# Products with the values in pairs of steps, scores four and maxima ten steps ahead, in an attention and mixture-of-experts block

## The reference

```
scores = (q @ k^T + q_rope @ k_rope^T) * scale      # 4 batches x 16 heads, 512 x 512
attn   = softmax(scores, axis=-1)
out    = (attn @ v) laid out by token @ Wout        # then x = x + ga * out
h      = layernorm(x) * (1 + cb) + sb
x      = x + gb * (experts(h) + shared(h))
```

## Time and profile before

| | us |
|---|---|
| median of 3 runs | 1003.52 (1001.63 to 1004.96) |
| the profiled execution | 1001.45 |
| its span | 999.6 |

### The profile page before, as it was taken

The page is one execution under the profiler, slowest core; times in us unless marked ns, Lnnn a source line. Parts: engine busy times, 40 slices in busy tenths (PEclk is TensorE's granted clock), DMA queues, the critical chain, the costliest instruction groups (busy, mean ns, idle before and its releaser), DMA issues.

```text
span 999.6 us, 19865 instructions
## 1 busy us (share of the span) xinstructions
PE 869.2 (87%) x6994; PEld 738.8 (74%) x6994; DVE 732.2 (73%) x1586; ACT 573.6 (57%) x1072; POOL 657.4 (66%) x625
## 2 busy tenths in 40 slices
PE   5788999999999999999999997649973999999940
PEld 5656777778788888788888786439862899999940
DVE  5777999887978788786879784676842566666648
ACT  1345777778787878887788886523310344444420
POOL 3555878878797888887887985515676355555530
PEclk9999999999999999999999999859985899999975
DMA  8661613233522345232334254333222333333337
GB/s 296 230 133 30 177 31 82 61 64 78 157 50 74 65 98 161 47 83 49 75 67 149 49 159 157 102 76 104 95 107 100 114 118 116 120 116 124 112 122 299
DMA packets 65756, 111.20 MB, mean 111 GB/s; under 512 B 16917, under 2 KB 43292, under 8 KB 63820
## 3 DMA queue, kind: packets, MB, share of 16 engines
q1 hardware_dynamic: 46905, 69.24, 26.0%
q10 hardware_dynamic: 11843, 22.84, 6.5%
q0 software_dynamic: 6912, 17.84, 4.6%
HBM read 46.06 MB, written 39.58 MB: 86 GB/s over the span
## 4 chain that ended last, share of the span: by engine, by line
PE 58%; DVE 11%; POOL 11%; DMA 10%; issue 5%; ACT 3%; SPq 0%; POOLq 0%; ACTq 0%; DVEq 0%
PE bank L680 12%; PE bank L682 11%; PE bank L681 10%; DMA slots<-h,slot_i 7%; PE bank L860 7%; PE bank L1076 7%; POOL p_lo L1912 5%; PE bank L837 4%; POOL turns L1890 2%; PE bank L1048 2%; POOL slots L1969 2%; PE bank L934 2%; DVE nmax L1250 1%; DVE turns L1224 1%; DVE turns L1223 1%
## 5 line engine op out<-in xcount | busy, mean ns | idle before, releaser
L1912 POOL TENSOR_TENSOR p_lo<-p_f,p_hi 128x512 f16<-128x512 f32 x256 | 329.6, 1299 | 46.7 <-ACT p_f L1647 45.8
L1644 ACT ACTIVATE p_hi<-bank,log_up 128x512 f16<-128x512 f32 x256 | 176.1, 688 | 108.2 <-PE bank L682 99.0
L1250 DVE TENSOR_REDUCE nmax<-bank 128x1 fp32r<-128x512 f32 x256 | 174.4, 686 | 86.1 <-PE bank L837 83.0
L1647 ACT ACTIVATE p_f<-bank,log_up 128x512 f32<-128x512 f32 x256 | 175.1, 684 | 15.2 <-POOL p_lo L1912 15.2
L860 PEld LDWEIGHTS bank<-vals,p_hi 128*128 128x128 f16 x2048 | 110.4, 98 | 59.6 <-POOL p_lo L1912 28.6
L860 PE MATMUL bank<-vals,p_hi 128*128 128x66 f16 x2048 | 138.7, 194 | 15.3 <-POOL p_lo L1912 15.1
L1230 DVE TENSOR_TENSOR qk<-rows_f,qk 128x512 fp32r<-128x512 f32 (+1 forms) x128 | 132.6, 1036 | 2.2
L1890 POOL TENSOR_TENSOR turns<-turns 128x512 f32<-128x512 f32 x64 | 90.4, 1414 | 66.0 <-DVE turns L1224 66.0
L680 PE MATMUL bank<-qk 128*128 128x512 f32 x256 | 122.2, 477 | 6.2 <-issue 4.9
L860 PE MATMUL bank<-vals,p_lo 128*128 128x66 f16 x1024 | 121.1, 193 | 0.0
L837 PE MATMUL bank<-qk 128*128 128x512 f32 x256 | 104.2, 410 | 3.8 <-DVE nmax L1250 3.4
(11 more groups left out here) (228 smaller groups left out, 2099.3 us busy)
## 6 DMA issues: line engine op xcount, KB each, us to landing
rows_f<-turns SPq DMA_DIRECT2D x64, 256.0 KB, 3.9
slots<-pad ACTq DMA_DIRECT2D x4, 2880.0 KB, 10.1
h<-slots SPq DMA_DIRECT2D x80, 144.0 KB
w_hi<-parts SPq DMA_DIRECT2D x16, 512.0 KB, 8.3
rows_f<-kl_f SPq DMA_DIRECT2D x32, 192.0 KB, 3.0
w_raw<-in_w ACTq DMA_DIRECT2D x4, 1408.0 KB, 11.8
h_dram<-h_hl SPq DMA_DIRECT2D x3, 1024.0 KB, 4.8
qk<-lat_st SPq DMA_DIRECT2D x16, 192.0 KB, 4.3
```

The costliest lines, as they stand in the source:

```text
L1250: dve.tensor_reduce(nmax[:, k % MAXES:k % MAXES + 1], max_bank[q % 2][:], AX_X, ALU.max, negate=True)\
L1644: act.activation(p_hi[:, u % TB, :], score_bank[u % 2][:], ACT.Exp, bias=log_up[:, 0:1], scale=SCALE)
L1647: act.activation(p_f[:, u % 2, :], score_bank[u % 2][:], ACT.Exp, bias=log_up[:, 0:1], scale=SCALE)\
L1912: pool.tensor_tensor(p_lo[:, u % TB, :], p_f[:, u % 2, :], p_hi[:, u % TB, :], ALU.subtract).then_inc(s_pl, 1)
```

## The change

TensorE makes the products with the values of steps `u` and `u + 1` together, at each even `u`, and none at odd `u`. The scores run four steps ahead in place of three, on TensorE, ScalarE and GpSimd; the maxima ten in place of nine, on TensorE and VectorE. Nothing else is changed, and no instruction is added or taken away.

```
-AHEAD = 3
-MAX_AHEAD = 2 * TB + 1
+AHEAD = 4
+MAX_AHEAD = 2 * TB + 2
...
             for w in range(AHEAD):
                 score(w)
             pe.wait_ge(spared, 3)
-            score_max(2 * TB)
+            for k in range(2 * TB, MAX_AHEAD):
+                score_max(k)
             aux(("kl", 2))
             pe.wait_ge(m_ev, 4)
             pe.wait_ge(v_l, 1)
             for u in range(UNITS):
-                weigh_values(u)
+                if u % 2 == 0:
+                    weigh_values(u)
+                    weigh_values(u + 1)
                 if u + AHEAD < UNITS:
                     score(u + AHEAD)
                 if u + MAX_AHEAD < UNITS:
...
             low_rows(2, 1)
             low_rows(2, 0)
-            row_max(2 * TB)
+            for k in range(2 * TB, MAX_AHEAD):
+                row_max(k)
             dve.wait_ge(p_hhi, NB)
```

## The result

The changed kernel took 1016.07 us (1014.14 to 1018.2), the kernel before 1003.78 us (1001.63 to 1004.96) in the same comparison: ratio 1.0134, interval 1.0111 to 1.0157. It is 1.3% slower. The prediction said 982.7 us, 976 to 997, and faster; the truth lies outside on the other side, where the prediction had put 0.08.

A forecast was written before the change was run, and what follows sets the result against it. TensorE's order of work was taken to bound the attention loop. Shorter score entries (10.1 us) plus removed waits on low probabilities (10.7) gave 20.8 us off the 1003.52 median: 982.7 us, range 976 to 997.

The forecast's parts named there:

- The entries of S: TensorE, 126 odd steps: first score product no longer follows short value products, 0.08 us each, 10.1 us saved.
- S: TensorE: the three score products of one step, 0.31 + 0.23 + 0.24 us from start to start.
- W: TensorE: the twelve products with the values of one step, 0.38 us; an ordinary entry shows a 0.22 us wait.
- M: TensorE: the one product for the maxima in a step, 0.23 us.
- rival B: TensorE: the 0.08 us per S does not come back; 992.8 us, chance 0.11.
- Queues: SP's queue: odd head's row of maxima, right behind the turned rows, lands in 1.9 us, hidden with 1.5 left.
- Rival E: SP's queue, 31 pairs: row of maxima lands late behind 256 KB; 15.5 us, 998, or some 1,033; chance 0.10.
- The 10.7 us of waits of W: Scores four ahead: of 15.2 us lost waiting for GpSimd's low probabilities, 10.7 go and 4.5 stay.
- Its three places in the batches: Once per batch four tiny GpSimd instructions delay the low products: 1.8 us lost each before, 1.5 after.
- Pressure of the pairs: W of odd steps wanted 0.38 us behind the even one, less room for scores and exponentials; taken as 0.
- rival C: Lost time moves: VectorE as late as before, odd W meets its low product; 993.4 us, chance 0.17.
- Maxima ten ahead: Extra S and M ahead of the loop hide in TensorE's 2.00 us wait; uncovered, 1.01 us once.

The follow-up runs named there:

- kernel 1: Changed kernel with the products with values one step at a time again, scores four and maxima ten ahead kept: 1021.07 us, ratio 1.0168.
- 10: Changed kernel, row of maxima first on SP's queue, GpSimd's first rotary sum one later: 997.72 us; also unpaired 999.99; paired with adds and deviations later 998.41.
- 9: Changed kernel with the row of maxima first on SP's queue, plus second adding of rows and deviations one step later: 997.14 us, ratio 0.9897.
- first kernel of 10: Changed kernel, still paired, with row of maxima first on SP's queue and GpSimd's first rotary sum one later: 997.72 us, ratio 0.9918.
- 6: Kernel before, scores three and maxima nine ahead, with value products of u-1 and u together at each odd u: 998.47 us, ratio 0.9954.
- 8: GpSimd's first rotary sum one later: in the kernel before with value products paired at odd steps 993.26 us; alone in the kernel before 996.0 us.
- 7: Changed kernel with row of maxima first on SP's queue and GpSimd's first rotary sum two steps later: paired 1005.14 us, unpaired 1004.58 us.
- experiment 2: Changed kernel with the odd head's row of maxima issued ahead of the turned rows on SP's queue: 1000.98 us, ratio 0.9971.

## Why the prediction was wrong, by its own steps

**The entries of S: right.** The page of after gives

```profile
L680 PE MATMUL bank<-qk 128*128 128x512 f32 x256 | 113.4, 443 | 20.5 <-issue 13.8
```

443 ns in the mean, 0.43 forecast, 479 in the unpaired kernel 1. (479 - 443) x 256 = 9.2 us for 10.1. From start to start, in the trace of after from 88 to 600 us outside the stretches at half clock, the median is 0.314 us in 102 places behind W, 0.231 in 67 behind L682 and 0.235 in 38 behind M. So rival B is out: behind 66-column products the first product of S costs more. The Trainium skill (TensorE: Matmul & The Clock Gate, Step-by-step: what each phase is for) would have the next weights load under the running product, and by that alone the term would be 0; these runs go against it there. That it is the load that costs the 0.08 was not shown by itself.

**Queues: the step that failed.** It said of the row of maxima "Hidden, with 1.5 us left". Its issue right behind the turned rows was foreseen, 0.6 us behind them. What was wrong is that 1.9 us, the median landing, was taken for every pair, and the times of one pair for all. Behind the 256 KB most rows of odd heads took 3.4 to 4.4 us, in the pair above 6.0. Rival E had this very mechanism, and priced it at 15.5 us: the waits of L680 on "issue" and on line 1233 grew by 20.4 - 5.5 = 14.9 us. That the two numbers agree is chance. It wasn't 0.5 us in each of 31 pairs but twelve waits: three of 2.3 to 2.7 us behind landings of 6.0 to 6.4, one of 4.2 behind 8.3 (in before it was 2.8, behind 8.2), and smaller ones between. With the clock behind them the late rows cost some 21 us, and not 15. Its chance of 0.10 was the error: the 1.9 of the earlier trace rows is a median over 64 issues. The instructions of L563 show how far it reaches, before and then after:

```profile
DMA to landing us min/median/max: 1.9/1.9/8.2
```
```profile
DMA to landing us min/median/max: 1.9/2.3/8.3
```

**The 10.7 us of waits of W: half right.** Four ahead does take them away where W is single (kernel 1: 5.9 us in 23). In pairs the second W waits: of the 11.5 us in 13 times, 10.9 in 10 times stand before a W right behind another, where the ordinary 0.22 does not arise. The prediction let 4.5 stay, so 7.0 too few. Its three places in the batches are there, right behind the deviations, with 1.8 us each. What it missed are the seven others, 5.5 us: it followed the low product of step 8p+9 through one pair, and there GpSimd's sum, in five of the seven an adding of rows as well (L1902), stands close ahead. Putting the sum one later took 9.2 of the 14.8 us away (10), the adds and deviations 3.7 (9).

**The granted clock: missing from the sum.** The earlier trace rows show 1.00 for the loop of before, and the prediction priced a late transfer at the lateness alone. Behind four of the new waits the clock was halved, 6.6 us. The Trainium skill (TensorE: Matmul & The Clock Gate, Part 1: The HAM clock gate) says that the array's clock is gated to half when TensorE idles and recovers with work; this trace agrees, 0.50 from inside a wait of 2.20 us to 3 us behind it, and shows that single waits inside a dense loop are enough. Not each does it: in kernel 1 a wait of 2.86 us (551.70 to 554.56) left the clock at 1.00 for the 3.4 us behind it, while in the first kernel of 10 it fell to 0.50 at 104.69, behind one of 1.46 us (102.36 to 103.82).

**Pressure of the pairs, rival C: partly right.** It was put at 0. In four comparisons of kernels with and without them the pairs gained 5.0 (after against 1), 5.5 (6 against before), 2.7 (8) and 2.3 us (10), and nothing with the sum two later (7). Never 10. The signs that C named, the same number of waits at even steps, did not come: W waited 13 times for 51. What grows with pairing, where the old waits are gone, are M's waits for reductions and S's. That fits the part of C on VectorE's pace; it was seen beside the edits and not changed by itself.

**Maxima ten ahead: no loss of its own shown.** Ahead of the loop it cost nothing, the first W starts at 86.32 against 87.18.

The account, from 980.65 forecast for the profiled execution to 1016.95: row of maxima 14.9, clock 6.6, second W 7.0, waits of L680 on turns, oT and exponentials 2.4 (2.4 + 1.6 + 1.3, against 0.6 + 1.7 + 0.6 before), behind the loop 3.8. Together 34.7 of 36.3 us. (The entries gave 0.9 less than forecast, and the loop began 0.9 earlier; the two cancel.)

**What stays open.** The 3.8 us behind the loop have no cause here. With the row first and the sum one later the changed kernel still takes 997.7 us and not 982.7. It still waits 11.3 us on "issue" before scores and 5.6 on low probabilities; and some two thirds of the shorter entries are eaten by small waits of S and M, of which no experiment took VectorE's part away alone. What decides whether the clock falls behind a wait is open too. The long landings are half explained. The three of 6.0 to 6.4 us in after (issued at 260.14, 401.89 and 543.23) all left while ScalarE's 2880 KB `slots<-pad` was under way and landed 1.4 to 2.5 us behind it; the one of 8.3 left among four loads of 1408 KB (`w_raw<-in_w`). With the row first on its queue, in experiment 2, the rows that left beside `slots<-pad` still took 5.2, 4.4 and 5.1 us, and the one beside `w_raw<-in_w` 8.3. So the place on the queue is 1.0 to 1.6 us of the first three and nothing of the last; the rest goes with the other traffic, which no run moved.

## What to carry to other kernels

A lookahead changed by one step changes which of two DMAs on a queue is ready first. For each queue, list what waits in front of each small urgent transfer after the change, and put the one that is due first ahead; that was worth 15 us here, and 7 us the other way round. Price such a transfer by its landing in the stretches where it shares the DMA engines, not by its median. For a stall of some 2 us on TensorE allow 1.5 to 1.7 us more: that is what each of the four here cost by the granted clock behind it, though other waits of this length cost nothing more.

## What the runs showed of the hardware

- A transfer of 2 KB with a median landing of 1.9 us took 3.4 to 4.4 us in most pairs where it was issued 0.6 us behind a 256 KB one on the same queue. It took 6.0 us (after, 401.89) with 256 KB ahead of it and a 2880 KB transfer of another queue under way, and 5.2 us (first kernel of 10, 255.69) with such a transfer under way and its own queue's 256 KB behind it.
- Behind waits of 1.86 us (at 211.03) and 2.20 us (at 405.81) the products ran at 0.43 us instead of 0.23 for about 3 us; the granted clock was 0.50 from 213.04 to 216.46 and from 407.60 to 411.02. Behind a wait of 1.48 us in the first kernel of 10 they ran at 0.24, and behind one of 2.86 us in kernel 1 the clock stayed at 1.00.
- The first score product costs 0.31 us from start to start behind products of 66 columns and 0.23 behind products of 512, in after; behind transposes of 128 columns it costs 0.31 too (kernel 6). Its mean duration is 476 to 479 ns in the unpaired kernels, 439 to 443 where W is paired at even steps, 452 and 453 where it is paired at odd ones.
